# Sums of exponentials moved to VectorE, finer waits, GpSimd held at normalisation, a tail of 1 MB loads, and new orders, in a perceiver block of six layers

## The reference, cut to what matters

```
x += softmax(q k^T / 16) v              # cross attention over the 257 rows, one head
x += causal self attention, 16 heads of 16
x += quantised gated FFN: w_down(silu(gate(xq)) * up(xq)), inputs rounded to 8 bits, weights to -1, 0, 1
x += latent attention over the 257 rows, 16 heads of 16      # "the second attention" over the context
x += self attention over 32 tokens, 16 heads of 64
x += routed FFN: 2 of 8 experts for each token, plus a shared gated FFN
```

## Time and profile before

| | us |
|---|---|
| median of three runs | 2981.65 |
| lowest, highest | 2981.3, 2986.57 |
| the profiled execution | 2995.97 |
| span of its trace | 2993.7 |
| TensorE busy (share of the span) | 2390.6 (80%) |
| VectorE busy | 1816.4 (61%) |
| ScalarE busy | 1208.3 (40%) |
| GpSimd busy | 493.8 (16%) |
| mean granted clock of TensorE | 0.942 of 2.4 GHz |

### The profile page before, as it was taken

The page is one execution under the profiler, slowest core; times in us unless marked ns, Lnnn a source line. Parts: engine busy times, 40 slices in busy tenths (PEclk is TensorE's granted clock), DMA queues, the critical chain, the costliest instruction groups (busy, mean ns, idle before and its releaser), DMA issues.

```text
span 2993.7 us, 94094 instructions
## 1 busy us (share of the span) xinstructions
PE 2390.6 (80%) x35446; PEld 1819.3 (61%) x35479; DVE 1816.4 (61%) x4744; ACT 1208.3 (40%) x3016; POOL 493.8 (16%) x614
## 2 busy tenths in 40 slices
PE   2788888888888888888888867888888888758882
PEld 2565666666566666666666656666666666646661
DVE  4566666666666666666666664566555555545555
ACT  1445555555555555455554551222222222212220
POOL 2111111111111111111111111111111111112220
PEclk9899999999999999999999988999999999979996
DMA  5011111111111111111111122000000000112225
GB/s 195 28 42 56 42 56 34 49 49 42 56 42 56 34 50 49 42 56 42 56 33 42 57 93 87 14 16 14 14 16 16 16 16 16 66 50 67 67 67 193
DMA packets 86060, 152.29 MB, mean 51 GB/s; under 512 B 11224, under 2 KB 39904, under 8 KB 84576
## 3 DMA queue, kind: packets, MB, share of 16 engines
q1 hardware_dynamic: 73136, 117.81, 12.5%
q0 software_dynamic: 6528, 17.87, 1.6%
q10 hardware_dynamic: 6192, 13.38, 1.2%
HBM read 120.40 MB, written 28.62 MB: 50 GB/s over the span
## 4 chain that ended last, share of the span: by engine, by line
issue 50%; PE 24%; DVE 9%; POOL 7%; ACT 4%; DMA 3%; DVEq 2%; SPq 0%; POOLq 0%; ACTq 0%
PE ps L385 16%; POOL mem L469 3%; PE ps L1193 2%; PE ps L1508 2%; POOL x L1065 2%; POOL rstd L1059 1%; PE ps L1145 1%; DVEq L1486 1%; DVE mem L1377 1%; DVE mem L1556 1%; DMA y_tok<-mem 1%; DVE mem L1351 1%; DVE mem L1407 1%; DVE mem L1408 1%; DVE mem L1411 1%
## 5 line engine op out<-in xcount | busy, mean ns | idle before, releaser
L791 ACT ACTIVATE mem<-ps 128x512 f32<-128x512 f32 (+6 forms) x800 | 436.6, 559 | 543.5 <-PE ps L385 260.7
L385 PE MATMUL ps<-mem 128*128 128x256 f16 (+1 forms) x4224 | 557.4, 290 | 119.0 <-DVE mem L1377 79.6
L385 PEld LDWEIGHTS ps<-mem 128*128 128x128 f16 x4224 | 422.3, 103 | 221.8 <-DVE mem L1377 83.1
L385 PE MATMUL ps<-xt,mem 128*128 128x128 f16 x4608 | 281.4, 220 | 29.0 <-DVE xt L1332 29.0
L385 PEld LDWEIGHTS ps<-xt,mem 128*128 128x128 f16 x4608 | 262.3, 98 | 42.4 <-DVE xt L1332 38.9
L841 ACT ACTIVATE mem<-ps,neg_max 128x257 f32<-128x257 f32 x512 | 237.4, 476 | 71.4 <-DVE neg_max L1028 71.4
L1059 POOL TENSOR_TENSOR rstd<-var_eps,neg_half 128x1 f32<-128x1 f32 x128 | 70.1, 548 | 1002.4 <-DVE var_eps L895 1002.4
L469 POOL TENSOR_TENSOR mem<-mem 128x514 f16<-128x514 f32 x136 | 160.7, 1184 | 368.3 <-ACT mem L464 368.3
L1028 DVE TENSOR_REDUCE neg_max<-ps 128x2 f32<-128x514 f32 x256 | 173.5, 688 | 58.4 <-PE ps L686 54.5
L1508 PE MATMUL ps<-mem 128*128 x576 | 156.5, 395 | 35.2 <-ACT mem L1534 34.7
L699 PE MATMUL ps<-cst,mem 128*128 128x128 f32 x1024 | 159.4, 284 | 12.5 <-ACT mem L841 12.5
(11 more groups left out here) (252 smaller groups left out, 4252.1 us busy)
## 6 DMA issues: line engine op xcount, KB each, us to landing
mem<-in_ctx_t SPq DMA_DIRECT2D x136, 257.0 KB, 2.7
mem<-in_ctx_n SPq DMA_DIRECT2D x136, 256.0 KB, 3.3
mem<-x_sorted SPq DMA_DIRECT2D x74, 128.5 KB, 2.1
mem<-y_pairs SPq DMA_DIRECT2D x32, 256.0 KB, 3.9
mem<-in_experts ACTq DMA_DIRECT2D x7, 768.0 KB, 8.7
x<-in_x_tok SPq DMA_DIRECT2D x34, 128.0 KB, 2.9
x_mid<-x SPq DMA_DIRECT2D x32, 128.0 KB, 1.7
x<-x_mid SPq DMA_DIRECT2D x32, 128.0 KB, 2.0
```

What stands on the lines that cost most here:

```text
L385: last = pe.matmul(dst, a, b, start=i == 0 and j == 0, stop=i == n - 1 and j == 2)
L791: act.activation(dst, src, ACT.Copy).then_inc(*did(done))
```

## The change

What it does:

- The exponentials of the fourth layer no longer give their sums; VectorE makes them in four reductions a tile over the stored exponentials, each over 4 x 257 columns.
- The 257th key's steps come later among the value steps.
- The quantised hidden rows are rounded, turned and copied in two halves; the down product's result moves to another part of bank 0.
- Several products of TensorE run the terms with the high part of an operand first, and wait for its low part only ahead of the others (`high_first`, the scores of the cross attention, the output product of layer five, the shared FFN's last product). Queries and keys of stage two exchange their banks.
- GpSimd waits after each power until the normalised rows are written.
- The tail loads the pairs in eight loads of 1 MB into buffers of their own, adds in place in instructions of 1024 columns, and stores 512 KB at a time. The pair rows and the output have a layout by partition for it; the host puts the output back.
- New strings for stage one, the joint and stage two.

```diff
-OUT_SLOTS = 4
+OUT_GROUPS = 8
+OUT_TILES = TILES // OUT_GROUPS
+OUT_WORDS = OUT_TILES * 2 * D
+OUT_AT = [OUT_WORDS * g for g in range(W_COLS[1] // OUT_WORDS)]
+OUT_AT += [EXPERTS_AT + OUT_WORDS * g for g in range(OUT_GROUPS - len(OUT_AT))]
+assert OUT_AT[-1] + OUT_WORDS <= EXPERTS_AT + EXPERTS * E_WORDS
...
 ORDER = {
     "first": dict(
-        tensor=("oooooyoyoyoyoooyooyoyoyooyoyyooyoooooyooyoooyoooooooooyoyyyoy"),
-        scalar=("oooyooyyoooyoyoooyoyoooyoooyyoooyoooyoyyooooooyyy"),
-        vector=("yoyyyyoooooyyooyyyoooooyoooooyoyyyyyoyooyyooyyoyyoyooyyoyyyyyyyyyyyyyoooyyyyyyyyyyo"),
-        gpsimd=("yyoooyooyyo"),
-        sync=("yyyyoyyoyyo"),
+        tensor=("ooooooyoyooyyooyoyoyoyoooyoyyooyooyoyoooyoooooooooooyoyyooyoyo"),
+        scalar=("oooooyoyyooyoyoyyooooooyooyyooyoooyoyoyoooooooyoyy"),
+        vector=("yyyyoyooooooyyyyyoyoooooooyoyoyoyyyoyooyyooyyoyyyooooyyoyoyyyyooyyyyyyyoyyyoyoyoyyyyyyyyo"),
+        gpsimd=("yoyoyooooyy"),
+        sync=("yyyoyyyoyyo"),
...
     "second": dict(
-        tensor=("ooyyyoyoyyyyyoyoyo"),
+        tensor=("oyoyyyoyyoyyyoyyoo"),
         scalar=("ooyooyooooyy"),
-        vector=("yyyyooyoyoooooyyoooyooyooooyyoooyyooyoooooooo"),
+        vector=("yyyyyooyoooooyoyoyooyoooooyyooooyyooyoooooooo"),
...
+        def high_first(pe, groups, low_there):
+
+            for part in range(2):
+                if part == 1:
+                    low_there()
+                for n, (dst, terms) in enumerate(groups):
+                    for i, (stands, moves) in enumerate(terms):
+                        for a, b in ([(stands[0], moves[0]), (stands[1], moves[0])], [(stands[0], moves[1])])[part]:
+                            last = pe.matmul(dst, a, b, start=(part == 0 and n == 0 and i == 0 and a is stands[0]),
+                                             stop=(part == 1 and n == len(groups) - 1 and i == len(terms) - 1))
...
-                need("hq")
-                for k in range(8):
-                    last = pe.transpose(ps[:, 0, k * 64:(k + 1) * 64].bitcast(BF16), hq[:, k * P:(k + 1) * P], identb[:, :])
-                last.then_inc(*did("hq_ps"))
-                yield
+                for half in range(2):
+                    need("hq", half + 1)
+                    for k in range(4 * half, 4 * half + 4):
+                        last = pe.transpose(ps[:, half, (k % 4) * 64:(k % 4 + 1) * 64].bitcast(BF16), hq[:, k * P:(k + 1) * P], identb[:, :])
+                    last.then_inc(*did("hq_ps"))
+                    yield
                 yield from keys_to_values(2)
-                need("hqt")
                 wt = ffn_w[:, 2, :].rearrange("p (k n) -> p k n", k=8)
                 for k in range(8):
-                    last = pe.matmul(ps[:, 1, 0:D], hqt[:, k], wt[:, k, :], start=(k == 0), stop=(k == 7))
+                    if k % 4 == 0:
+                        need("hqt", k // 4 + 1)
+                    last = pe.matmul(ps[:, 0, D:2 * D], hqt[:, k], wt[:, k, :], start=(k == 0), stop=(k == 7))
...
-                yield from last_turned()
                 for v in range(UNITS):
                     yield from values(v)
                     if v + 2 < UNITS:
                         yield from turned(v + 2)
                     if v == 1:
+                        yield from last_turned()
+                    if v == 3:
                         yield from last_values()
-                    if v == 3:
+                    if v == 5:
...
-                        act.activation(prob4[:, u, i], ps[:, 2 * c + i, 0:KEYS], ACT.Exp, bias=neg_max[:, u, i:i + 1],
-                                       accum_out=sums[:, 0, 2 * u + i:2 * u + i + 1]).then_inc(*did("exp4"))
+                        act.activation(prob4[:, u, i], ps[:, 2 * c + i, 0:KEYS], ACT.Exp, bias=neg_max[:, u, i:i + 1]).then_inc(*did("exp4"))
...
-                ins = yield from normalise(3, x[:, :])
-                yield from then(ins)
+                yield from normalised(3, x[:, :])
+                need("xn3")
...
-                yield from then(dve.tensor_scalar(rq3, r3, small[:, 15:16], ROUND, ALU.mult, ALU.add))
-                dve.tensor_scalar(hq, rq3, ROUND, 127.0, ALU.subtract, ALU.min).then_inc(*did("hq"))
-                yield
+                for i in range(2):
+                    cols = slice(512 * i, 512 * (i + 1))
+                    yield from then(dve.tensor_scalar(rq3[:, cols], r3[:, cols], small[:, 15:16], ROUND, ALU.mult, ALU.add))
+                    dve.tensor_scalar(hq[:, cols], rq3[:, cols], ROUND, 127.0, ALU.subtract, ALU.min).then_inc(*did("hq"))
...
-                need("exp4", 2 * UNITS)
+                for w in range(4):
+                    need("exp4", 4 * w + 4)
+                    dve.tensor_reduce(sums[:, 0, 4 * w:4 * w + 4], prob4[:, 2 * w:2 * w + 2].rearrange("p u i m -> p (u i) m"), X, ALU.add).then_inc(*did("sum4"))
+                    yield
+                need("sum4", 4)
...
             def power(pool, t, n):
                 pool.wait_ge(*at(t, f"ln_var{n}"))
                 pool.tensor_tensor(rstd[:, :], var_eps[:, :], neg_half[:, :], ALU.pow).then_inc(*did(f"ln_rstd{n}"))
+                pool.wait_ge(*at(t, f"xn{n}"))
...
-                pe.wait_ge(*at(t, f"xt{n}_lo"))
+                pe.wait_ge(*at(t, f"xt{n}_hi"))
...
-                    bank = ps[:, g % 2]
-                    by_feature_pair(pe, bank[:, 0:D], w2("aq", C, WIDE), xt_p, range(2 * g, 2 * g + 2))
-                    by_feature_pair(pe, bank[:, D:2 * D], w2("ak", C, WIDE), xt_p, range(2 * g, 2 * g + 2)).then_inc(*did("qk5_ps"))
+                    groups = []
+                    for j, name in enumerate(("aq", "ak")):
+                        hi, lo = w2(name, C, WIDE)
+                        for i in range(2):
+                            oc = slice((2 * g + i) * P, (2 * g + i + 1) * P)
+                            groups.append((ps[:, 1 - g % 2, D * j + P * i:D * j + P * (i + 1)], [((hi[:, kc, oc], lo[:, kc, oc]), (xt[:, 0, kc], xt[:, 1, kc])) for kc in range(C)]))
+                    high_first(pe, groups, lambda: need("xt5_lo")).then_inc(*did("qk5_ps"))
...
-                need("o5_lo", 2)
+                need("o5_lo", 1)
+                need("o5_hi", 2)
                 ao_hi, ao_lo = w2("ao", 8, D)
-                last = product(pe, ps[:, 0, 0:D], [((o5[:, 0, k], o5[:, 1, k]), (ao_hi[:, k], ao_lo[:, k])) for k in range(8)])
+                for part in range(2):
+                    if part == 1:
+                        need("o5_lo", 2)
+                    for k in range(8):
+                        for weight in (ao_hi, ao_lo)[0:2 - part]:
+                            last = pe.matmul(ps[:, 0, 0:D], o5[:, part, k], weight[:, k], start=(part == 0 and k == 0 and weight is ao_hi), stop=(part == 1 and k == 7))
...
-            with sp.Fori(0, TILES // OUT_SLOTS) as t:
-                for k in range(OUT_SLOTS):
-                    sp.wait_ge(s["out_pair"], t * OUT_SLOTS + k + 1)
-                    sp.sem_inc(s["may_load"], 1)
-                    sp.dma_start(out_pair[:, k].rearrange("p k n -> p (k n)"),
-                                 pair_rows[bass.ds(t * (OUT_SLOTS * 2 * P) + k * 2 * P, 2 * P), :].rearrange("(p k) n -> p (k n)", k=2)).then_inc(s[f"pairs_in{k}"], 16)
-            for k in range(OUT_SLOTS):
-                sp.wait_ge(s[f"out_done{k}"], 16 * (TILES // OUT_SLOTS) + 1)
+            by_token = pair_rows[0:PAIRS, :].rearrange("(p r) n -> p (r n)", p=P)
+            for g in range(OUT_GROUPS):
+                sp.dma_start(out_pair[g].rearrange("p s k n -> p (s k n)"), by_token[:, OUT_WORDS * g:OUT_WORDS * (g + 1)]).then_inc(s[f"pairs_in{g}"], 16)
+            sp.wait_ge(s["out_done"], 16 * OUT_GROUPS)
...
+            for g in range(OUT_GROUPS):
+                act.wait_ge(s["out_sum"], g + 1)
+                act.dma_start(out[:, OUT_TILES * D * g:OUT_TILES * D * (g + 1)], out_pair[g][:, :, 0, :]).then_inc(s["out_done"], 16)
...
+            for g in range(OUT_GROUPS):
+                one, other = out_pair[g][:, :, 0, :], out_pair[g][:, :, 1, :]
+                stored = base[:, OUT_TILES * D * g:OUT_TILES * D * (g + 1)].rearrange("p (s n) -> p s n", s=OUT_TILES)
+                dve.wait_ge(s[f"pairs_in{g}"], 16)
+                dve.tensor_tensor(one, one, other, ALU.add).then_inc(s["out_pair"], 1)
+                dve.wait_ge(s["out_pair"], g + 1)
+                dve.tensor_tensor(one, one, stored, ALU.add).then_inc(s["out_sum"], 1)
```

90 lines of the change are left out of this document (45 added, 45 removed).

## The result

The kernel after takes **3088.29 us** (median of four runs, 3078.39 to 3093.43) beside 2984.11 for the kernel before on the same chip: a ratio of 1.0329, 95% interval 1.0304 to 1.0353 (the quotient of these two medians is 1.0349, inside it). It is slower, as forecast, but by 104 us where the forecast had 46, and the time lies above the range. Of the four runs that give 3038.66 in experiment 4, the one of 3066.03 was a slow one: it is in the median but not in the ratio, and the waits quoted there are from its trace.

A forecast was written before the change was run, and what follows sets the result against it. TensorE, the busiest engine, bounds stage one, more than half the span. Stage one +37, stage two +14 and tail -5 sum to +46: profiled 2995.97 becomes 3042, median 2981.65 becomes 3028 us; range 2955 to 3075.

The forecast's parts named there:

- the ledger of waits: Stage one: new waits of 5.9 us less 5.4 removed, +0.5, taken as +0.6 a tile with longer issue.
- First, the 2.3 us gap stays: Stage one, TensorE's wait for the second normalisation: +0.6 - 0.5, about 0 change a tile.
- Second, a new gap of 2.4: Stage one, eighth score step: waits for the sixth exponential pair, which ScalarE's order puts behind the self attention's exponential.
- Third, a new gap of 2.0: Stage one, ahead of the output product: waits for the selection, now later in VectorE's order; 4.5 - 2.5 = 2.0 us.
- Fourth, 1.5 in four short waits: Stage one: 0.4 before turning probabilities, 0.2 and 0.5 at ScalarE's copies, 0.5 at sums ahead of the selection.
- I take 0.4 more, +0.6: Stage one: 0.4 more clock drops a tile than the 0.9 before, costing +0.6 us a tile.
- The price of a drop: Stage one: 1.5 us each, reading the disturbed tile's 3.1 us excess (clock 0.94, not 1.00) as two drops.
- the clock falls at every gap: Rival, chance 0.13: three clock drops a tile in stage one, 79 us at most, half counted, giving 3070 us.
- Stage two: Product behind the attention starts 2.1 us later, next product +0.3, a moved gate 0.15: 31 x 0.45 = +14 us.
- partly at the lower level: Stage two, product behind the attention: 3.85 us, between 2.8 at the full clock level and 4.3 as profiled.
- Tail: Final transfers: 47 us becomes 42 at 376 GB/s, -5 us, bounds -11 and 0.
- sums collide with GpSimd: Rival, chance 0.05: GpSimd's last context subtraction, 1.12 us, falls beside the first sum; 31 x 1.1 = 34, 3062 us.

The follow-up runs named there:

- experiment 4: Kernel after, ScalarE's sixth exponential pair earlier: 3092.29 us; with former stage-two strings, TensorE's two turns ahead of the self attention's turn: 3038.66; both moves, former strings: 3018.09.
- experiment 1: Kernel after plus unread filler products on TensorE in four waits of stage one (12, 18, 36, 30): 2976.33 us, ratio 0.9948.
- experiment 5: Kernel after with the former TensorE and VectorE strings of stage two: 3012.06 us, ratio 1.0069.
- experiment 6: Kernel before with only the new tail: 2984.56 us beside 2991.67, ratio 0.9975.
- experiment 3: Kernel after with the sums back on ScalarE's accumulators: 3090.49 us; the same edit on the 2883.42 us kernel with fillers and former stage-two strings: 2881.71.
- experiment 7: Kernel before plus fillers: 2936.45 us; kernel after plus fillers, former stage-two strings: 2883.42; that without GpSimd's wait: 2907.42; or with two order moves, fewer fillers: 2869.99.

## Why the prediction failed, by its own steps

The direction was right. The size was wrong, and the step that failed is the number of low stretches a tile. A second error, in the ledger of waits, ran the other way and hid part of the first.

- **The waits of stage one.** "First, the 2.3 us gap stays": 0.92 + 1.30 = 2.2, at the second and third score steps instead of the normalisation, so this size was right by luck. "Second, a new gap of 2.4": 2.48. "Third, a new gap of 2.0": 2.08. "Fourth, 1.5 in four short waits": 0.17. So the two new long ones were right and the short ones were not there; the idle time of a tile changed by -1.09 instead of +0.6, within 31 tiles 52 us less than the term. The reason given for the second was half right: experiment 4 shows that the chain behind it comes out elsewhere when one step of ScalarE's order is moved.
- **The clock of stage one: the step that failed.** "I take 0.4 more, +0.6" a tile. Measured: +2.95 busy a tile with the same instructions, 2.35 more than the term, 73 us. The price of a drop was right: against the 43.21 busy of the undisturbed tile, 47.50 - 43.21 = 4.29 for 2.97 low stretches is 1.44 each, where the prediction had 1.5, and the disturbed tile does hold two of them. The number before was right too, 0.83 for 0.9. The number after was wrong: 0.9 + 0.4 = 1.3 was a guess without a row, and the trace has 2.97, one behind nearly every long wait; the granted clock went from 0.97 to 0.88. Filling the waits took all of them away and 3.6 us a tile (experiment 1). The rival that said so ("the clock falls at every gap", 0.13, 3070) had the number exactly, "three drops a tile"; I gave it too little chance. By the measured parts, -1.09 + 2.95 = +1.86 a tile, 57.7 us where I had 37.
- **Stage two.** Forecast +14, measured +46.5. The mechanism stands in the trace as written: the power released by the scatter, the turned rows ahead of the product, 3.96 us of wait. The failed term is again the clock: I took 3.85 us for the product, "partly at the lower level", and it took 5.15, 1.30 more, and busy time rose by 1.01 a tile. Here it is not the number that grew: both kernels have 29 low stretches in 29 tiles, but with 112.7 us at the lower level before and 198.0 after. Experiment 5 shows that the rest of the change gained 1.35 a tile, near the 0.65 + 0.94 that I counted for the finer waits, and that the new strings gave back 2.85. Over both stages the clock was thus taken too low by some 73 and 40 us; the ledger of stage one gave back 52, the rest of stage two 8 and the tail 5, which leaves the 48 between 94 and 46.
- **Tail.** -5 forecast, -10.3 in the traces and -7 in experiment 6, near its bound of -11 in the traces. The whole tail moved 355 GB/s. DMA: Bandwidth & Descriptors of the Trainium skill (section Bandwidth) gives 341 for a load of 1 MB; with several in flight this trace shows a little more.
- **The sums** cost 0, as the ledger had it (experiment 3). The rival "sums collide with GpSimd" fell: in the tile above, GpSimd's subtraction of 1.12 us runs from 351.17 to 352.29, beside the first of three sums that take 3.47 together from 351.38, 1.16 each on average, where one alone takes 1.21:

```profile
351.38 3.47 DVE L1059 TENSOR_REDUCE sums<-mem 128x4 f32<-128x1028 f32 x3
355.79 1.21 DVE L1059 TENSOR_REDUCE sums<-mem 128x4 f32<-128x1028 f32 x1
```

```profile
351.17 1.12 POOL L486 TENSOR_TENSOR mem<-mem 128x514 f16<-128x514 f32 x1 [3.99 <-ACT mem L481]
```

  By SBUF — State Buffer of the Trainium skill (section Who interferes with whom) a reduction never contends for the port pair on this chip; these rows agree.
- **GpSimd's hold.** I took 0.8 a tile off in stage one; experiment 7 gives 24 / 31 = 0.8, and normalised rows of 0.41 with the hold beside a mean of 0.71 without it. Right.

Against the before profile the sum was 37 + 14 - 5 = 46, and the spans gave 57.7 + 46.5 - 10.3. What remained of the difference of the medians, 104 against 93, is the before profile's 12 us over its median.

## What to carry to other kernels

A wait of TensorE can have two prices: its own length, and the slower clock of the products behind it, here 1.4 us of busy time for each low stretch. So before an order is changed, list the places where TensorE will stand still for 1 us or more, and work out the time once with a low stretch behind each of them: fewer and shorter waits in sum are no gain if more of them bring one. How many will, these runs do not let one foretell: 24 low stretches came with 29 waits of 2.3 us and as many of 1.4 before, 86 with the three groups of waits after, and a filler in one wait also cleared stretches behind others. If a wait can't be covered by real work, filler products with unread results are cheap to try: 3.6 us a tile here, for 96 products in time that was idle.
